# Second attention of a two-block model: attention-row transposes behind the second score half, VectorE's small chains laid between each other

## What is computed

```python
x = x + tanh(g_xattn[0]) * attention0(layernorm(x), ctx, ctx)
x = x + tanh(g_ffn[0])   * top2_of_8_experts(layernorm(x))
x = x + tanh(g_xattn[1]) * attention1(layernorm(x), ctx, ctx, bias)   # the change is in this stage
x = x + tanh(g_ffn[1])   * slot_experts(x)      # its first half, slot attention, runs in the same loop

def attention1(q, k, v, bias):                  # per tile: 128 rows, 16 heads of 16
    s = einsum('bhqd,bhkd->bhqk', q @ Wq, k @ Wk) / 4 + bias
    return (softmax(s) @ (v @ Wv)) @ Wo
# slot attention: softmax over the tokens of (slot queries . layernorm-free x keys), per tile,
# with its maximum, exponentials, normalisation, transposed weights and value product
```

## Time and profile before

| | us |
|---|---|
| median of 3 runs | 1302.65 (1301.74 to 1304.87) |
| the profiled execution, its own time | 1301.76 |
| its span in the profile | 1300.0 |
| TensorE busy | 1263.5 (97%) |
| VectorE busy | 879.6 (68%) |
| ScalarE busy | 798.6 (61%) |
| GpSimd busy | 746.0 (57%) |

### The profile page before, as it was taken

How to read it: one execution, slowest core, us unless ns; L and a number is a source line. 1 busy time by engine, 2 the same in 40 slices (tenths; PEclk the granted TensorE clock), 3 DMA queues, 4 the chain that set the end, 5 groups by cost and what they waited for, 6 DMA issues and landing times.

```text
span 1300.0 us, 38189 instructions
## 1 busy us (share of the span) xinstructions
PE 1263.5 (97%) x14749; PEld 1129.6 (87%) x14749; DVE 879.6 (68%) x2366; ACT 798.6 (61%) x1741; POOL 746.0 (57%) x833
## 2 busy tenths in 40 slices
PE   9999999998999999999999998999999999999898
PEld 8888898886999999999999977889999998655476
DVE  5778888876665565556555037999999997321387
ACT  5666777664777777778775446666666665322454
POOL 2678888764777877787775044566666653100131
PEclk9999999999999999999999999999999999999999
DMA  6675555642777767776776711631111112599812
GB/s 219 239 246 180 193 195 173 208 164 93 263 227 236 218 212 226 225 224 216 229 234 229 312 50 46 225 114 52 51 51 55 51 51 79 204 427 426 331 59 74
DMA packets 103891, 237.51 MB, mean 183 GB/s; under 512 B 8992, under 2 KB 86176, under 8 KB 91296
## 3 DMA queue, kind: packets, MB, share of 16 engines
q1 hardware_dynamic: 97568, 218.29, 49.1%
q0 software_dynamic: 6144, 16.79, 4.0%
HBM read 174.22 MB, written 60.82 MB: 181 GB/s over the span
## 4 chain that ended last, share of the span: by engine, by line
PE 88%; DVE 5%; DMA 3%; issue 2%; ACT 1%; POOL 0%; SPq 0%; ACTq 0%; PEldq 0%; DVEq 0%; POOLq 0%
PE ps L2173 13%; PE psT L2158 7%; PE ps L716 6%; PE psS L693 5%; PE ps L1101 5%; PE psT L702 4%; PE ps L1043 4%; PE ps L2158 3%; PE psS L2158 3%; PE ps L1026 2%; PE ps L1060 2%; PE ps L966 2%; PE psT L708 2%; DMA arena<-wset_dram 2%; PE ps L2414 2%; PE ps L727 2%
## 5 line engine op out<-in xcount | busy, mean ns | idle before, releaser
L2126 POOL TENSOR_TENSOR wb_lo<-arena,wb_hi 128x2048 fp32r<-128x2048 f32 x64 | 296.8, 4638 | 93.3 <-ACT wb_hi L2249 93.3
L2173 PE MATMUL ps<-wb_hi,hT_hi 128*128 128x256 f32 x528 | 152.3, 288 | 0.4 <-DVE hT_lo L2304 0.4
L702 PE MATMUL psT<-arena 32*128 32x128 f32 x2048 | 148.5, 283 | 0.4 <-ACT arena L1278 0.4
L2173 PE MATMUL ps<-wb_lo,hT_hi 128*128 128x256 f32 x528 | 147.8, 280 | 0.0
L2173 PE MATMUL ps<-wb_hi,hT_lo 128*128 128x256 f32 x528 | 147.6, 280 | 0.0
L693 PE MATMUL psS<-arena 32*128 32x256 f32 x1024 | 138.2, 387 | 0.8 <-ACT arena L1357 0.4
L2249 ACT CAST wb_hi<-arena 128x1024 fp32r<-128x1024 f32 x128 | 130.7, 1045 | 13.4 <-DMA arena<-w_dram 13.4
L702 PEld LDWEIGHTS psT<-arena 32*128 32x128 f32 x2048 | 124.1, 186 | 1.1 <-issue 0.6
L1724 POOL TENSOR_TENSOR arena<-arena,eps_sb 128x1 f32<-128x1 f32 x94 | 23.6, 252 | 146.8 <-DVE arena L1595 106.5
L2314 DVE TENSOR_TENSOR arena<-ps,arena 128x512 f32<-128x512 f32 (+1 forms) x39 | 25.4, 651 | 115.0 <-PE ps L2173 74.6
L693 PEld LDWEIGHTS psS<-arena 32*128 32x128 f32 x1024 | 92.4, 185 | 11.6 <-issue 6.1
(11 more groups left out here) (528 smaller groups left out, 3871.8 us busy)
## 6 DMA issues: line engine op xcount, KB each, us to landing
arena<-wset_dram SPq DMA_DIRECT2D x24, 2048.0 KB, 15.0
xs_rows<-arena SPq DMA_DIRECT2D x33, 1024.0 KB, 5.9
arena<-w_dram SPq DMA_DIRECT2D x32, 1028.0 KB, 5.9
arena<-w_dram SPq DMA_DIRECT2D x32, 1024.0 KB, 5.9
arena<-w_dram SPq DMA_DIRECT2D x7, 2052.0 KB, 12.9
w_sb<-xs_rows SPq DMA_DIRECT2D x33, 256.0 KB, 2.8
xs_rows<-arena SPq DMA_DIRECT2D x33, 256.0 KB, 5.6
arena<-ctxT_dram SPq DMA_DIRECT2D x63, 128.0 KB, 3.3
```

The costliest lines, as they stand in the source:

```text
L702: nc.tensor.matmul(psT[:, b, j * P:(j + 1) * P], kbd_[p, (k - 1) % NK, c, par, :], qT[p, (k - 1) % 3, c, :], start=j == 0, stop=False, ski ...
L2126: nc.gpsimd.tensor_tensor(wb_lo[:, u % 2, part], wb_raw[:, u % 2, part], wb_hi[:, u % 2, part], ALU.subtract).then_inc(w_g.sem, 1)
L2173: last = nc.tensor.matmul(ps[5][:, t * D:(t + 1) * D], hp[:, f, t * P:(t + 1) * P], wp[:, f, :], start=f == 0 and t == 0 and n == 0, stop= ...
```

## The change

Three things are moved, and nothing is added or removed. On TensorE the transposes of `att` go from ahead of the second score half to behind it. On VectorE the first moments of tile k-3 go between the reciprocal and the product that make `att`; the two slot maxima and their negation go one by one into the split of the maxima; and the subtraction that makes `aT_lo` goes from ahead of the maximum over the second score half to behind the split. All other orders stay.

```diff
 # tensor, step k
-                    if not A and valid(k - 2):
-                        pe.wait_ge(out_v.sem, out_v.at(k - 2, "att"))
-                        for c in range(C):
-                            last = nc.tensor.transpose(ps[7][:, c * P:(c + 1) * P], ...
-                        last.then_inc(o_p.sem, 1)
...
                     scores(k, 1)
...
-                    if not A and k == B:
-                        last_tiles(pe)
-                        break
-                    if A and valid(k - 2):
+                    if valid(k - 2):
                         pe.wait_ge(out_v.sem, out_v.at(k - 2, "att"))
...
+                    if not A and k == B:
+                        last_tiles(pe)
+                        break
 # vector: new functions
+                def attention_rest(i):
+                    dve.wait_ge(av_a.sem, av_a.at(i, "aT"))
+                    before(dve, o_p.sem, o_p.at(i - 1, "O"))
+                    nc.vector.tensor_tensor(aT_lo[:, :, :], ps[7][:, 0:D].rearrange("p (c t) -> p c t", c=C),
+                                            aT_hi[:, :, :], ALU.subtract).then_inc(aT_v.sem, 1)
+
+                def slot_maximum(i, c):
+                    if c == 0:
+                        dve.wait_ge(x1_p.sem, x1_p.at(i, "s"))
+                        before(dve, x2_v.sem, x2_v.at(i - 1, "pn"))
+                    nc.vector.tensor_scalar(sc[:, c, :], ps[4][:, c * P:(c + 1) * P], qac[:, c:c + 1], None,
+                                            ALU.add, ALU.max, accum_out=smx[:, c:c + 1]).then_inc(x1_v.sem, 1)
+
+                def slot_negated(i):
+                    dve.wait_ge(x1_v.sem, x1_v.at(i, "s1"))
+                    nc.vector.tensor_scalar(snx, smx, -1.0, None, ALU.mult).then_inc(x1_v.sem, 1)
 # vector, step k
+                    if not A and valid(ln_i):
+                        dve.wait_ge(out_v.sem, out_v.at(ln_i, "x"))
+                        nc.vector.bn_stats(stat[:, 1, :], x_all[:, ln_i + 1]).then_inc(n4_v.sem, 1)
                     if valid(out_i):
                         dve.wait_ge(out_v.sem, out_v.at(out_i, "den"))
...
-                    if not A and valid(ln_i):
-                        dve.wait_ge(out_v.sem, out_v.at(ln_i, "x"))
-                        nc.vector.bn_stats(stat[:, 1, :], x_all[:, ln_i + 1]).then_inc(n4_v.sem, 1)
...
-                    if not A and valid(out_i):
-                        dve.wait_ge(av_a.sem, av_a.at(out_i, "aT"))
...
                     if not A and k == B:
+                        attention_rest(out_i)
                         last_tiles(dve)
                         break
...
+                        if not A and valid(rt_i):
+                            slot_maximum(rt_i, 0)
                         dve.wait_ge(mx_v.sem, mx_v.at(k, "hi"))
                         nc.vector.tensor_tensor(mrest, mx, m2[:, :, 0, :], ALU.subtract).then_inc(mx_v.sem, 1)
...
+                        if not A and valid(rt_i):
+                            slot_maximum(rt_i, 1)
                         dve.wait_ge(mx_v.sem, mx_v.at(k, "rest"))
                         nc.vector.tensor_copy(m2[:, :, 1, :], mrest).then_inc(mx_v.sem, 1)
...
+                        if not A and valid(rt_i):
+                            slot_negated(rt_i)
                         dve.wait_ge(mx_v.sem, mx_v.at(k, "mid"))
                         nc.vector.tensor_tensor(m2[:, :, 2, :], mrest, m2[:, :, 1, :], ALU.subtract).then_inc(mx_v.sem, 1)
...
-                    if not A and valid(rt_i):
-                        dve.wait_ge(x1_p.sem, x1_p.at(rt_i, "s"))
...
+                    if not A and valid(out_i):
+                        attention_rest(out_i)
```

More of the change, by code:

```diff
@@ L997, in tensor @@
                         input_turned(k + 1)
-                    if not A and valid(k - 2):
-                        pe.wait_ge(out_v.sem, out_v.at(k - 2, "att"))
-                        for c in range(C):
-                            last = nc.tensor.transpose(ps[7][:, c * P:(c + 1) * P],
-                                                       att[:, c * HC:(c + 1) * HC, :].rearrange("p h d -> p (h d)"), cv["ident"])
-                        last.then_inc(o_p.sem, 1)
                     if not A and k == -1:
@@ L1625, in vector @@
                             nc.vector.tensor_reduce(slot_i[:, :, sl_i], ohp2, AX, ALU.add).then_inc(rk_v.sem, 1)
-                    if not A and valid(out_i):
-                        dve.wait_ge(av_a.sem, av_a.at(out_i, "aT"))
-                        before(dve, o_p.sem, o_p.at(out_i - 1, "O"))
-                        nc.vector.tensor_tensor(aT_lo[:, :, :], ps[7][:, 0:D].rearrange("p (c t) -> p c t", c=C),
-                                                aT_hi[:, :, :], ALU.subtract).then_inc(aT_v.sem, 1)
                     if not A and k == B:
+                        attention_rest(out_i)
                         last_tiles(dve)
```

## The result

The changed kernel takes 1333.95 us (median of 6 runs, 1330.77 to 1337.22) against 1301.45 us before (6 runs, 1299.88 to 1304.87); the ratio is 1.0248, with a 95% interval of 1.0233 to 1.0262. It is 32.5 us slower; 27.5 were forecast. The profiled execution took 1334.45 us, its span is 1332.7.

The account below looks back on a forecast made before the run. TensorE, busy for 97% of the span, was taken as the bound. Steps 4 to 9 (6.7 us), steps 2, 3 and 31 (2.1) and 10 to 30 (18.7) add 27.5 to 1301.8: 1329 us, range 1314 to 1338.

Parts of the forecast that it names:

- steps 4 to 9: Short steps of the second attention: late `aT_lo` makes each 11.15 us instead of 10.04, 6 x 1.11 = 6.7 us.
- steps 10 to 27: Long steps, priced within steps 10 to 30: each 11.55 us instead of 10.66, 0.89 us more.
- a step lasts at least until the output product starts, and 4.4 us more: Second attention: TensorE works 4.4 us without pause from output product to next first score half, so VectorE's next maximum waits.
- GpSimd's hold: `x_lo` delays VectorE's subtraction in short steps (0.40 us) and cast in long ones (0.89 us growth instead of 0.60).
- Rival (a): GpSimd's `x_lo` misses VectorE's split because its own chain shifts: 1321 us, chance 0.22.
- No term below is for the clock: TensorE's clock was 1.00 in all three windows, with and without gaps, so the forecast gave it no time.
- VectorE sets the pace of the short steps: VectorE is busy 48.58 of 50.19 us in five short steps, so these 10.04 us steps go by its pace.
- rival (b): Small instructions don't overlap as assumed (11 us more), or a second GpSimd instruction is met: about 1340 us, chance 0.10.
- The removed wait: TensorE's transposes no longer wait for `att`: 10.6 us in all, 0.78 in a full short step, already in the sum.
- Rivals (c) and (d): (c): `aT_lo` in time, only the removed wait counts, 1295 us, chance 0.04. (d): no change, near 1302 us, chance 0.03.
- Steps 2, 3 and 31: Steps with fewer slot instructions or no keys, priced at the unhindered short step's 0.7 us each: 2.1 us.
- The new wait: TensorE's output product waits for `aT_lo` in some 30 steps, 0.5 to 1.2 us each.

Follow-up runs that it names:

- e1: The changed kernel with the subtraction that makes `aT_lo` directly behind the second maximum, other moves kept: 1297.24 us against 1300.69 before the change, ratio 0.9966.
- e2: The kernel before, with only TensorE's transposes of `att` moved behind the second score half: 1306.63 us, ratio 1.0038.
- e5: The changed kernel, with GpSimd's `x_lo` made to wait until VectorE's split of the maxima is finished: 1322.95 us, ratio 1.0160.
- e6: The changed kernel, with eight products of constants on TensorE ahead of the output product in steps 2 and 3: 1331.09 us, ratio 1.0227.
- e3: The kernel before, with only VectorE's slot maxima and moments interleaved, `aT_lo` still ahead of the second maximum: 1301.91 us against 1300.69, ratio 1.0014.
- e7: The kernel before, with late transposes and `aT_lo` directly behind the second maximum, moments and slot maxima in their old places: 1298.53 us against 1301.32, ratio 0.9977.

## Why the prediction was right, step by step

The median lies inside the range and 5 us above the forecast. The mechanism is the forecast one: `aT_lo` comes late, the output product waits for it, and each step grows by that. The span grew by 32.7 us; it splits like this, by the first maxima of both traces, with 0.4 us more ahead of step 2.

| part | predicted | measured |
|---|---|---|
| steps 2 and 3 | 1.4 | 19.95 - 16.84 = 3.1 |
| steps 4 to 9 | 6.7 | 1.2 + 5.6 = 6.8 |
| steps 10 to 27 | 18 x 0.89 = 16.0 | 207.19 - 191.82 = 15.4 |
| steps 28 to 30 | 2.7 | 35.59 - 32.08 = 3.5 |
| step 31 and all behind it | 0.7 | 219.1 - 215.5 = 3.6 |

- **The rule "a step lasts at least until the output product starts, and 4.4 us more"** gave the step wherever the output product waited for `aT_lo`, from step 5 on: +7.11 and 4.40 in the changed kernel's long step, +5.17 and 4.41 in e1's short one. In e2 it was only a lower bound (5.1 to 5.7 us behind the output product, since VectorE came later). In steps 2 and 3, which have fewer products, the rest was 3.3 us in e1, not 4.4.
- **Two small errors met.** With `aT_lo` laid out by durations of the earlier trace rows, the sum gave 11.15 us for a short step (measured 11.15) and 11.55 for a long one (11.51). That it fits to 0.04 us is partly luck: `aT_lo` ended 0.08 to 0.10 us earlier than laid out (+6.61 and +6.97 against +6.69 and +7.07), and TensorE took 0.14 us to start behind it instead of the 0.06 read from the transposes.
- **GpSimd's hold** was met where it was forecast, the subtraction in short steps and the cast in long ones, and e5 took it away: 0.4 us a short step, 0.26 a long one. Rival (a), in which it is missed, fell.
- **"No term below is for the clock" failed.** It was drawn from windows in which TensorE waited for up to 1 us at a time. In the changed kernel's trace the clock fell right behind the wait of 2.02 us in step 3, and that step took 10.8 us against e6's 9.2: 1.6 us. The stretch behind step 31 may be worth another 1.5 us (219.1 us against e6's 1328.8 - 1111.2 = 217.6), by one pair of traces. Together that would be more than half of what the forecast lacked. All six executions of the changed kernel had a mean clock below 1.00 (0.994 to 0.999), where 18 of the 31 timed beside the experiments for the kernel before were at 1.00; so part of such a loss is in the medians too.
- **"VectorE sets the pace of the short steps" was half the truth.** Its 48.58 busy us of 50.19 suggested it, and the wait for `att` looked like slack. e3 gave VectorE time and the step grew with `att`; e2 took the wait away and the step shrank by 0.10 us only. Two loops of nearly the same length, 10.04 through `att` and 9.94 of VectorE's own work, lay on top of each other: each relief alone bought 0.10 us or less a step; the transposes late and `aT_lo` directly behind the second maximum bought 0.28 (e7), the parted chains on top of that 0.47 (e1). It did not hurt the forecast, since a third loop, through `aT_lo`, became longer than both.
- **Steps 28 and 29** took 11.9 and 12.2 us: there GpSimd's next addition follows `x_lo` at once, as in the earlier trace rows, and holds the subtraction too. This is part of rival (b), in 2 steps instead of all.
- **Small terms.** The removed wait vanished as said, and brought nothing. Rivals (c) and (d) needed `aT_lo` 0.6 to 0.7 us earlier than the shortest chain; e1 shows that they were one instruction's place away.
- **Steps 2, 3 and 31** were priced at 0.7 us each. Step 2 grew by 0.9 us and step 3, at full clock in e6, by 0.6. Step 31 did more: its output product starts 1.2 us later (+5.94 against +4.74), its cast and subtraction being held (0.36 and 0.50 us), and the wait there is 1.73 us where the kernel before waited 0.99 for `att`. By the output product of step 32 the changed kernel is 2.0 us late, and so is e6, at full clock; the rest of the 3.6 us comes behind it.
- **Signs read off wrongly.** The new wait was forecast at 0.5 to 1.2 us in every step. It is 0.68 in long steps but 1.66 in short ones: that range was the growth of the step, and in short steps the wait for `att` of 0.78 us, which is gone, comes back at the output product. TensorE's share of the long steps is 94%, not 92%.

What stays open: why the clock falls where it does, and how much of the 32.5 us it makes in the executions that were not traced.

## What to carry to other kernels

When an instruction is moved behind others on one engine, write down when its consumer wants it and lay out the new chain by start-to-start times; the wait that the move removes says nothing about this (0.78 us here, which only moved to the output product). Moving a producer without its consumer is the first thing to suspect: here the split and the slot maxima could stay interleaved and the transposes late, if only `aT_lo` stood ahead of them (e1, 0.34% faster than before). And where an engine is 97% busy and another one waits, there may be two loops of equal length; test by giving each its relief alone and both together.

## What the runs showed of the hardware

- VectorE casts and subtractions of 128x16 elements that take 0.17 us alone take 0.4 to 0.65 beside a 128x256 two-input instruction of GpSimd that began first; in the changed order this was 8.7 us in steps 4 to 30 (after against e5), and 11 us between the medians.
- TensorE's granted clock was 0.50 (1.2 GHz) for some 3 us in three places of the changed kernel's trace, and 1.00 (2.4 GHz) wherever else it worked. Behind the wait of 2.02 us in step 3, 32 products took 1.94 us instead of 1.08. With the waits of steps 2 and 3 filled by products of constants it stayed at 1.00 there, in one trace. Long waits are neither needed nor enough: it fell at 298.3 us behind waits of at most 0.46, and held 1.00 through waits of 1.66 us in each short step and, in e6, through one of 1.88.
- A VectorE instruction that doesn't depend on the one before it starts about 0.07 us before that one's end in the trace, one that does 0.03 behind it; with the chains parted, busy time fell by 0.37 us a step (e7 against e1).
